# Query spread between the first projection tiles, projection in two banks, and the exponential unit on transposed features, in a two-layer graph network

## The reference

```python
h = relu(layernorm(x));  x = x + gcn(h, W) + b               # gather over edges, weights by degree
h = relu(layernorm(x))
for layer in (1, 2):                                          # 4 heads, then 1 head
    xr = einsum('nd,rdf->rnf', h, W_l)                        # three projections, one per edge type
    a  = leaky_relu(xr[type, dst] @ q + xr[type, src] @ k)    # a score per edge and head
    e  = exp(a - segment_max(a, dst)[dst])
    h  = segment_sum(e / segment_sum(e)[dst] * xr[type, src], dst) + b_l
    if layer == 1: h = elu(h)
x = x + h
```

## Time and profile before

| | |
|---|---|
| median of 3 executions | 1744.78 us (1741.37 to 1746.79) |
| profiled execution | 1749.11 us, span 1747.2 us, mean granted clock 0.912 |
| first layer's gather | about 255 to 511 us of the span |
| layer 1: query spread, projection and maxima, gather | 523.7 to 565.1, 568.7 to 875, 885 to 1173.5 us |
| layer 2: the same | 1201.4 to 1241.8, 1244.9 to 1504.8, 1511.6 to 1740 us |

### The profile page before, as it was taken

How to read it: one execution, slowest core, us unless ns; L and a number is a source line. 1 busy time by engine, 2 the same in 40 slices (tenths; PEclk the granted TensorE clock), 3 DMA queues, 4 the chain that set the end, 5 groups by cost and what they waited for, 6 DMA issues and landing times.

```text
span 1747.2 us, 27255 instructions
## 1 busy us (share of the span) xinstructions
PE 1544.5 (88%) x6490; PEld 901.4 (52%) x6494; DVE 998.5 (57%) x2491; ACT 183.2 (10%) x360; POOL 1054.2 (60%) x1190
## 2 busy tenths in 40 slices
PE   3787969999987997999879988876899999899997
PEld 1343635555547554666545544443555556455553
DVE  8899653454540888888867776551443543222332
ACT  0210111111110111011100011112011111000000
POOL 2682546665535778887167655432677775377674
PEclk9897989999995999889989999886699999899999
DMA  6322049887740113111178866552113113489897
GB/s 229 120 98 82 37 167 338 285 264 241 233 133 3 46 48 101 30 38 38 37 254 277 268 224 208 181 158 70 20 47 110 47 38 56 163 305 299 286 301 268
DMA packets 86645, 268.61 MB, mean 154 GB/s; under 512 B 31867, under 2 KB 32242, under 8 KB 86582
## 3 DMA queue, kind: packets, MB, share of 16 engines
q0 software_dynamic: 51840, 199.49, 37.1%
q1 hardware_dynamic: 34742, 68.32, 10.9%
HBM read 236.18 MB, written 31.57 MB: 153 GB/s over the span
## 4 chain that ended last, share of the span: by engine, by line
PE 61%; POOL 15%; issue 8%; DMA 7%; DVE 7%; ACT 1%; DVEq 1%; SPq 0%; POOLq 0%; PEldq 0%; ACTq 0%
PE ps L1121 14%; PE ps L1161 11%; PE ps L1092 11%; POOL ring L438 10%; PE ps L1163 6%; PE ps L1164 5%; PE ps L1007 3%; PE ps L1034 3%; DMA ring<-rows,idxr 2%; PE ps L1037 2%; DVE stage L666 2%; PE ps L1050 2%; POOL ring L411 2%; DMA ring<-rows,idx 1%; DMA ring<-rows,idxs 1%
## 5 line engine op out<-in xcount | busy, mean ns | idle before, releaser
L1121 PE MATMUL ps<-wreg,hT 128*128 128x384 f32 x1440 | 486.4, 500 | 7.5 <-PEq L1114 6.6
L438 POOL DMA_INDIRECT ring<-keys,idxr x360 | 383.9, 1066 | 167.0 <-issue 110.2
L411 POOL DMA_INDIRECT ring<-rows,idxr x304 | 300.1, 987 | 218.9 <-PE ps L1161 82.6
L1121 PEld LDWEIGHTS ps<-wreg,hT 128*128 128x128 f32 x1440 | 280.5, 196 | 202.2 <-issue 22.8
L1161 PE MATMUL ps<-ring,zw 128*128 x664 | 240.4, 523 | 26.6 <-DVE zw L911 26.5
L1092 PE MATMUL ps<-ring,zw 128*128 x664 | 235.1, 499 | 18.8 <-DVE zw L744 18.7
L841 DVE TENSOR_TENSOR hn<-hn,al 128x1024 f32 (+1 forms) x166 | 137.5, 828 | 119.5 <-POOL al L449 79.3
L411 POOL DMA_INDIRECT ring<-rows,idx x152 | 146.1, 961 | 96.2 <-PE ps L1092 82.1
L1161 PEld LDWEIGHTS ps<-ring,zw 128*128 128x128 f32 x664 | 133.3, 204 | 131.7 <-issue 69.0
L909 DVE TENSOR_TENSOR ring<-ring,al x166 | 159.3, 960 | 42.8 <-SPq L328 24.8
L1092 PEld LDWEIGHTS ps<-ring,zw 128*128 128x128 f32 x664 | 114.3, 191 | 93.7 <-issue 49.6
(11 more groups left out here) (175 smaller groups left out, 1340.5 us busy)
## 6 DMA issues: line engine op xcount, KB each, us to landing
wreg<-in_L_gnn_W SPq DMA_DIRECT2D x12, 2304.0 KB, 10.6
rows<-stage SPq DMA_DIRECT2D x30, 386.0 KB, 2.6
rows<-stage SPq DMA_DIRECT2D x30, 384.5 KB, 3.0
ring<-keys,idxr POOLq DMA_INDIRECT x360, 2.6
ring<-rows,idxr POOLq DMA_INDIRECT x304, 4.6
rows<-wreg SPq DMA_DIRECT2D x10, 384.0 KB, 3.1
xs<-in_x SPq DMA_DIRECT2D x3, 1152.0 KB, 10.3
out_x<-xs SPq DMA_DIRECT2D x9, 384.0 KB
```

Source lines behind the costliest of these rows:

```text
L411: nc.gpsimd.indirect_dma_start(ring[:, t % (2 * RING), 0:WIDTH[l]], None, rows[l], bass.IndirectOffsetOnAxis(idx[:, t:t + 1], 0)).then_inc ...
L438: nc.gpsimd.indirect_dma_start(kb[:, n % KSEMS, t % KB, 0:4], None, keys[l], bass.IndirectOffsetOnAxis(idxr[:, t:t + 1], 0)).then_inc(k_in ...
L1121: last = mm(ps[:, 2 * (nt % 2) + h, 0:HALF], hT[:, k, nt * P:(nt + 1) * P], wreg[:, r % 2, k, h * HALF:(h + 1) * HALF], start=(k == 0), st ...
```

## The change

There are four parts. (1) The projection uses two banks, 0 and 1, and TensorE may be two halves ahead of ScalarE (`CREDIT`). (2) The query spread of node tile 0 stands behind projection tile 0, that of tiles 1 and 2 behind projection tile 1, and that of tiles 3 to 9 behind projection tile 2, in both layers; TensorE's wait for spread_read moves to the start of relation 1. (3) GpSimd asks for three batches of keys ahead instead of two, and each key transfer waits until the one four before it has landed. (4) In layer 1, TensorE transposes the divided sums before bias and elu; the bias is then a number per partition (`b1c`, loaded at the start and negated once), and ScalarE does both parts of the elu from PSUM in 12 activations of 128 columns and one exponential; VectorE's bias addition is gone and its last elu operation works on hT. The transposes come one tile sooner.

```diff
-KSEMS = 3
+KSEMS = 4
+KAHEAD = 3
+KFLIGHT = 4
+CREDIT = 2
+SPREAD_AFTER = {1: {0: (0,), 1: (1, 2), 2: (3, 4, 5, 6, 7, 8, 9)}, 2: {0: (0,), 1: (1, 2), 2: (3, 4, 5, 6, 7, 8, 9)}}
...
+                sp.dma_start(b1c[:, 0, :], bd[1].rearrange("(k p) -> p k", p=P)).then_inc(s_b1, 16)
...
-                        nc.gpsimd.indirect_dma_start(kb[:, n % KSEMS, t % KB, 0:4], None, keys[l], bass.IndirectOffsetOnAxis(idxr[:, t:t + 1], 0)).then_inc(k_in[l][n % KSEMS], 16)
+                        if t >= KFLIGHT:
+                            pool.wait_ge(k_in[l][t % KFLIGHT], 16 * (t // KFLIGHT))
+                        nc.gpsimd.indirect_dma_start(kb[:, n % KSEMS, t % KB, 0:4], None, keys[l], bass.IndirectOffsetOnAxis(idxr[:, t:t + 1], 0)).then_inc(k_in[l][t % KFLIGHT], 16)
...
-                ask_keys(0)
-                ask_keys(1)
+                for n in range(KAHEAD):
+                    ask_keys(n)
                 pool.wait_ge(qs_ready, l)
                 for n in range(KBATCHES):
                     score(n)
-                    if n + 2 < KBATCHES:
-                        ask_keys(n + 2)
+                    if n + KAHEAD < KBATCHES:
+                        ask_keys(n + KAHEAD)
...
-                        copy_t(NW + 2 * NT + nt, hT[:, :, nt * P:(nt + 1) * P]).then_inc(t_free, 1)
+                        n = NW + 2 * NT + nt
+                        act.wait_ge(t_ready, n + 1)
+                        if nt >= 1:
+                            act.wait_ge(h2_ready, nt)
+                        for k in range(KT):
+                            last = nc.scalar.activation(etmp[:, k * P:(k + 1) * P], tbuf(n)[:, k * P:(k + 1) * P], ACT.Relu, bias=b1c[:, 1, k:k + 1], scale=-1.0)
+                        last.then_inc(elu_neg, 1)
+                        for k in range(KT):
+                            last = nc.scalar.activation(hT[:, k, nt * P:(nt + 1) * P], tbuf(n)[:, k * P:(k + 1) * P], ACT.Relu, bias=b1c[:, 0, k:k + 1])
+                        last.then_inc(t_free, 1)
+                        act.wait_ge(elu_neg, nt + 1)
+                        nc.scalar.activation(etmp[:, :], etmp[:, :], ACT.Exp, scale=-1.0).then_inc(elu_exp, 1)
...
-                        act.wait_ge(elu_in, j + 1)
                         if j >= 1:
-                            act.wait_ge(hn_ready, 2 * NT + j)
-                        nc.scalar.activation(etmp[:, :], hn[:, j % 2, :], ACT.Relu, scale=-1.0).then_inc(elu_neg, 1)
-                        act.wait_ge(elu_neg, j + 1)
-                        nc.scalar.activation(etmp[:, :], etmp[:, :], ACT.Exp, scale=-1.0).then_inc(elu_exp, 1)
-                        if j >= 2:
-                            node_tile(j - 2)
+                            node_tile(j - 1)
...
-                def add_bias(j):
-                    if j == 0:
-                        dve.wait_ge(s_bias[1], 16)
-                    dve.wait_ge(divided, j + 1)
-                    V.tensor_tensor(hn[:, j % 2, :], hn[:, j % 2, :], bias[:, :], ALU.add).then_inc(elu_in, 1)
...
-                            if j >= 2:
-                                elu(j - 2)
-                            add_bias(j - 1)
+                            if j >= 3:
+                                elu(j - 3)
...
-                spread_open(BANK_Q, SQ)
-                for j in range(NT):
-                    spread(j, q16, BANK_Q, R * H, SQ)
-                spread_close(BANK_Q, SQ, q_spread[l])
-                pe.wait_ge(spread_read, 2 * l - 1)
-                pe.sem_inc(stage_in[l], 4)
+                pe.sem_inc(stage_in[l], CREDIT)
...
                     for nt in range(NT):
                         project(r, nt)
+                        if r == 0 and nt in SPREAD_AFTER[l]:
+                            spread_queries(SPREAD_AFTER[l][nt])
...
-                    if l == 1 and j >= 3:
-                        for nt in ([j - 3] if j < NT else [j - 3, j - 2, j - 1]):
+                    if l == 1 and j >= 2:
+                        for nt in ([j - 2] if j < NT else [j - 2, j - 1]):
                             to_features(2, nt)
```

More of the change, by code:

```diff
@@ L178, in gnn_kernel @@
         stats = sb("stats", [P, 2, 6])
+        b1c = sb("b1c", [P, 2, KT])
         mv = sb("mv", [P, NT, 2])
@@ L247, in gnn_kernel @@
         qs_ready = sem("qs_ready")
-        k_in = {l: [sem(f"k_in{l}_{i}") for i in range(KSEMS)] for l in (1, 2)}
+        k_in = {l: [sem(f"k_in{l}_{i}") for i in range(KFLIGHT)] for l in (1, 2)}
         k_sum = {l: sem(f"k_sum{l}") for l in (1, 2)}
@@ L293, in _ @@
                     sp.dma_start(qk1[:, :, a, :], v.rearrange("(t p) h -> p t h", p=P)).then_inc(s_qk, 16)
+            with nc.allow_non_contiguous_dma(reason="a small vector"):
+                sp.dma_start(b1c[:, 0, :], bd[1].rearrange("(k p) -> p k", p=P)).then_inc(s_b1, 16)
             def prepare_load(l, r, buf):
@@ L548, in _ @@
                     W = HALF // 2 + 1
+                    act.wait_ge(s_b1, 16)
+                    nc.scalar.activation(b1c[:, 1, :], b1c[:, 0, :], ACT.Copy, scale=-1.0).then_inc(b1_neg, 1)
+                    act.wait_ge(b1_neg, 1)
                     def node_tile(nt):
@@ L869, in sums @@
                     dve.wait_ge(w_used[l], 2 * bnd[j + 1] + 2 * RING)
+                    if l == 1 and j >= 1:
+                        dve.wait_ge(divided, j)
                     bk = 2 * (j % 2)
@@ L924, in _ @@
                 if l == 1:
+                    elu(NT - 2)
                     elu(NT - 1)
@@ L1067, in to_features @@
                         by_node(l, nt // 2 - 1)
-                pe.wait_ge(hn_ready, l * NT + nt + 1)
-                pe.wait_ge(t_free, n if l == 1 else n - 1)
+                if l == 2 and nt % 2 == 1 and nt >= 3:
+                    by_node(l, nt // 2 - 1)
+                if l == 1:
+                    pe.wait_ge(hn_ready, NT + nt + 1)
+                    pe.wait_ge(t_free, n)
+                else:
+                    pe.wait_ge(divided, nt + 1)
+                    pe.wait_ge(t_free, n - 1)
                 for k in range(KT):
@@ L1072, in to_features @@
                 last.then_inc(t_ready, 1)
-                if l == 2 and nt % 2 == 0 and nt >= 2:
-                    by_node(l, nt // 2 - 1)
             pe.sem_inc(w_used[0], 2 * RING)
@@ L1104, in _, with spread_queries @@
                 by_node(l, NT // 2 - 1)
-                pe.wait_ge(q16_ready, l)
-                pe.wait_ge(st_tail, 2 * (SPREAD - 1))
-                spread_open(BANK_Q, SQ)
-                for j in range(NT):
-                    spread(j, q16, BANK_Q, R * H, SQ)
-                spread_close(BANK_Q, SQ, q_spread[l])
-                pe.wait_ge(spread_read, 2 * l - 1)
-                pe.sem_inc(stage_in[l], 4)
+                pe.sem_inc(stage_in[l], CREDIT)
+                def spread_queries(tiles):
+                    if tiles[0] == 0:
+                        pe.wait_ge(q16_ready, l)
+                        pe.wait_ge(st_tail, 2 * (SPREAD - 1))
+                        spread_open(BANK_Q, SQ)
+                    for j in tiles:
+                        spread(j, q16, BANK_Q, R * H, SQ)
+                    if tiles[-1] == NT - 1:
+                        spread_close(BANK_Q, SQ, q_spread[l])
+                if not SPREAD_AFTER[l]:
+                    spread_queries(range(NT))
                 def project(r, nt):
@@ L1120, in project @@
                         for k in range(KT):
-                            last = mm(ps[:, 2 * (nt % 2) + h, 0:HALF], hT[:, k, nt * P:(nt + 1) * P], wreg[:, r % 2, k, h * HALF:(h + 1) * HALF], start=(k == 0), stop=(k == KT - 1))
+                            last = mm(ps[:, h, 0:HALF], hT[:, k, nt * P:(nt + 1) * P], wreg[:, r % 2, k, h * HALF:(h + 1) * HALF], start=(k == 0), stop=(k == KT - 1))
                         last.then_inc(p_ready, 1)
```

34 lines of the change are left out of this document (20 added, 14 removed).

## The result

The changed kernel takes **1735.04 us** (median of 7 executions, 1732.76 to 1741.42), the kernel before in the same session 1744.78 (median of 7). The ratio is 0.9953, interval 0.9935 to 0.9972: faster by about half a per cent. The prediction was 1756 us with a range from 1743 to 1770, so it missed, and the sign was wrong. The profiled execution took 1734.29 us, span 1732.4, against 1749.11 and 1747.2.

A forecast was written before the change was run, and what follows sets the result against it. The prediction took VectorE's chain after the query spread to bound layer 1's projection stage, and TensorE layer 2's. 1 + 24.6 - 32 + 3 + 15 = +11.6, taken as +11 on 1744.8, gave 1756 us, range 1743 to 1770.

The forecast's parts named there:

- Layer 1's gather: Layer 1's gather: tile-end pauses and the low clock behind them mostly go, less work moved in; -32 us, bounds -16 and -38.
- Query spread, layer 1: Layer 1's projection stage: three projection tiles ahead of the spread's end delay scores and VectorE's chain; +24.6 us, bounds 20 and 28.
- Layer 2: Layer 2's projection stage: spread and scores 25 us later, TensorE waits at the maxima's transposes; +15 us, bounds 10 and 21.
- End of the gather: End of layer 1's gather: ScalarE's activations for the last tiles are no longer covered; +3 us, bounds 0 and 7.
- Start: Kernel start: b1c is one more small strided load ahead of the first weights; +1 us, bounds 0 and 5.6.
- Two banks: Projection: ScalarE's copy of a half lies wholly under the next half, so using two banks costs 0.
- The third batch: GpSimd's key loads: falls into the longer spread and does not shorten VectorE's chain; no separate term in the sum.
- (a): Both projection stages: TensorE paces them, so later scores cost nothing; -31, 1714 us; 7 in 100.
- (b): Maxima: the third batch of keys gives VectorE back its 11.0 us of waits for scores; 1745 us; 15 in 100.
- (c): Layer 1's gather: the transfers become the bound; +11 + 16, 1772 us; 14 in 100.
- (d): Projection: two banks stall it, 0.5 us for each of 60 halves in layer 2; +30, 1786 us; 5 in 100.

The follow-up runs named there:

- e10: Kernel of e6 plus one VectorE reduction over 768 columns per tile end, behind the wait for the division: 1785.68 us, ratio 1.0228.
- e7: Changed kernel with by_node put back at the tile end of its by_query, behind the transposes: 1738.14 us, ratio 0.996 to the kernel before.
- e4b: Changed kernel with VectorE again waiting for the division of the same tile before scaling the next rows: 1739.44 us, ratio 0.9973 to the kernel before.
- e5: Changed kernel with ScalarE's division put back behind TensorE's transposes of the same tile end: 1754.5 us, ratio 1.0055 to the kernel before.
- e6: Changed kernel with VectorE's wait for the division and the division behind the transposes both put back: 1772.87 us, ratio 1.0155 to the kernel before.
- e8: Changed kernel with the edits of e6 and e7 together: 1773.92 us, ratio 1.0158 to the kernel before.
- e9: Changed kernel with layer 2's query spread put back ahead of the projection, layer 1's still interleaved: 1724.35 us, ratio 0.9869 to the kernel before.
- e2b: Changed kernel with the query spread of both layers put back ahead of the first projection tile: 1703.67 us, ratio 0.9785 to the kernel before.
- e1b: Kernel before with part (4) of the change alone: 1704.17 us, ratio 0.9781 to the kernel before.
- e1: Kernel before with part (4) alone, in the first session: 1937.12 us against 1964.77, ratio 0.9874.
- e2: Changed kernel with both layers' query spread back ahead of the projection, in the first session: 1962.81 us, ratio 1.002 to the kernel before.
- e11: Changed kernel with the added VectorE instruction of e10 per tile end and no wait put back: 1741.05 us, ratio 0.9982 to the kernel before.

## Why the prediction was wrong

The steps were these: start, query spread of layer 1, gather, its end, layer 2, two banks. All mechanisms were found in the profile after. The sizes were not right, and all five sized terms erred to the same side: by 1.4, 3.4, 15.8, 2.0 and 3.8 us, 26.4 together, of which the gather is 60%. That turns +11.6 into -14.8.

**The step that failed is "Layer 1's gather", -32 us, which measured -47.8, beyond its own bound of -38.** The mechanism was right and the term was mis-sized. Its idle part was put at 13.2 + 8 = 21.2 us and measured 29.7. I counted the pauses of six tile ends and left out those of the first two, 2.3 us each, which went too (the sum names them only in the bound of -38). I also left 0.5 to 0.6 us of idle at each of the six, after the first layer's; after the change there is none. Together that is 4.7 + 3.4 = 8.1 of the 8.5. Its clock part was put at 15 us. TensorE's busy time fell 18.2 with 3.6 us of work added, so it was about 22; at the same work e10, which has the old pauses, is busy 256.5 - 236.5 = 20.0 us more than the changed kernel. At the six starts that I charged, equal numbers of gather matmuls took about 16 us more before than after, so their price was nearly right. About 2.1 us more stand at the two starts that I left out, and 1.5 in tile 0; the rest is in no single place. Work moved in was put at 4 and is 3.6, since no `by_node` came into the loop.

The size can be read from the granted clock alone. At a mean of 0.92 over 289.4 us (e10) the engine is at the lower level for (1 - 0.92) / 0.5 = 0.16 of the time, 46 us, and loses half of that, 23; at 0.99 over 240.7 us it loses 2.4; the difference is 20.8 against the 20.0 measured. For the kernel before it is 23.1 - 2.4 = 20.7 against about 22. A hundredth of the granted clock is 2.9 us here, so the agreement is no closer than that. The Trainium skill reckons in this way (TensorE: Matmul & The Clock Gate, section "HAM oscillation — how this bites in real kernels"): the extra is the time at the low clock times 1 - 1.2/2.4. By this the trace agrees. Had I put the 0.92 of the whole gather into it at once, 0.08 x 288.5 = 23 us would have stood where 15 did.

**Which edit did it** was named only half rightly. The prediction said that VectorE no longer waits for the division, that the division is no longer late, and that `by_node` stands later. The third is worth nothing (e7). Put back into the changed kernel, the first alone costs about 4 us (e4b), the second alone 17 (e5), both 29 (e6). The last 20 come with what I costed at nothing in its own right: the bias addition, 0.96 us of VectorE that stood in the one place where transposes, division, VectorE and TensorE followed one another. An instruction of its length in its place costs them (e10). That the copy behind the exponential (4.51 us twice) went with the free ScalarE fits e7 and e8, but no kernel put the old exponential back by itself.

**Query spread, layer 1**: +24.6, measured +21.2. The three tiles, two of them slow, took 28.2 us for 26.9. But the spread's own pieces became shorter. Stretches of the spread, TensorE before, layers 1 and 2:

```profile
523.73:565.10 41.37, 35.21 (x618) 0.50 0.09 3
1201.41:1241.80 40.39, 32.82 (x210) 0.57 0.12 3
```

and after, the three pieces of layer 2:

```profile
1181.40:1191.11 9.71, 8.25 (x67) 0.70 0.20 42
1201.24:1206.91 5.67, 4.76 (x49) 0.89 0.25 71
1217.67:1232.69 15.02, 12.44 (x97) 0.67 0.13 29
```

Before, the whole spread ran at a granted clock of 0.50 and 0.57. Behind projection tiles its pieces run at 0.67 to 0.89, and take 30.4 instead of 40.4 us in layer 2 (in layer 1 38.0 instead of 41.4, at 0.64 to 0.73). Of the 10.0 us in layer 2, 7.4 are busy time and 2.6 idle time. I had charged the interleaving for tiles that start slow behind a piece of spread and not credited it for pieces that start fast behind a tile. The section of the Trainium skill that the prediction named here (TensorE: Matmul & The Clock Gate, "HAM oscillation — how this bites in real kernels") tells of the first of these only, blocks that start slow behind a pause. The trace has both: 4.9 us lost on the two slow tiles of layer 2, and 10.0 won on its pieces. What the interleaving costs, 20.7 us in layer 1 and 10.7 in layer 2, stands in TensorE's waits at the maxima instead, 22.0 us more in layer 1 and 17.1 us that are new in layer 2, since the scores come later.

**Layer 2**: +15, measured +11.2 (e9: 10.7). The scores moved by 17 us and not by 25, for the reason just named. TensorE's waits at the maxima are new, as forecast, but 17.1 us in all (10.0 and 7.1) where 6 to 13 stood. That the term still ended inside its bounds (10 to 21) is in part luck: the shorter pieces of the spread, which the sum did not have, took back more than the longer waits cost.

**End of the gather** +3, measured +1. All of its parts but one came out a little shorter: 6.1 us to the first `by_query` (sum: 6.6), then 5.29 for it (5.0), 10.8 to the second (11.7), and 4.8 for that and what follows (5.9). **Start** +1, measured -0.4: the projection of layer 1 starts at 520.9 in the changed kernel and between 520.0 and 522.9 in the eight kernels made from it that keep layer 1's interleaving, so this is no difference. **Two banks** 0: right (e2b). **The third batch**: "falls into the longer spread", right, and e2b shows what it costs without that cover.

Of the rivals none came true. (a) is refuted by e9 and e2b: later scores cost 20.7 and 10.7 us. (b) would need shorter waits for scores; they are 10.7 us after 11.0. (c) would need transfers that hold TensorE up in the gather; it moved 299 GB/s in a middle tile and TensorE was busy all of it. (d): e2b.

A version that beats both kernels is therefore part (4) without the interleaving: 1704.17 us (e1b) or 1703.67 (e2b), 2.2% under the kernel before. In the first session e1 was 1.3% under it and e2 level with it, so only part (4) alone was faster in both.

## What to carry to other kernels

Where several engines hand over to one another at the end of a loop, write down that chain first; an instruction of 1 us in it made TensorE's pause 1 us longer and its clock lower behind it, 2.5 us here for each 1 us (19.6 us for eight of them, e10), while the same instruction beside the chain cost little or nothing (e11). If a gain and several losses are all estimated, ask whether they err to the same side: here each cost was taken from the middle of its bounds and came out near its lower end. And run a bundle's parts alone: the bundle's 0.5% was a gain of 2.2% less a loss of 1.7%.

## What the runs showed of the hardware that was not expected

**A short pause and a slightly longer one differ by more than their length.** At tile ends with 1.55 + 1.34 us idle (e6) the granted clock of the next tiles was 0.93 to 1.00, with 1.55 + 2.33 us (e10) 0.82 to 0.93. With 1.55 us alone (e5) the whole gather stood at 0.99.

**The same program took 12.6% longer in another session** (1964.77 against 1745). e1 and e1b are one kernel, and their spans are 1933.7 and 1700.7 us; of the 233 us between them 159 lie between layer 1's gather and layer 2's, 496.6 instead of 337.9. Stretches of TensorE in layer 2's projection in e1, in the first session:

```profile
1275.00:1320.00 45.00, 44.49 (x130) 0.93 0.16 37
1320.00:1470.00 150.00, 58.66 (x80) 0.53 0.09 11
```

and the same stage in e1b:

```profile
1200.00:1467.00 267.00, 256.26 (x951) 0.96 0.23 62
```

For 150 us TensorE is nearly all the time at the lower clock, with gaps between single matmuls in which no other engine is waited for; in e1b the stage has nothing of the kind. VectorE too idles in these 150 us without a wait that the profile shows, 77.8 us before its running maximum (L850). Gathers are 12 to 16 us longer there too (256.1 against 244.2 in e1 and e1b). Why is open: nothing was tried that tells the clock, the supply of instructions and the chip apart.
